# A decoder layer's mLSTM groups: row factors on GpSimd, values centred on VectorE, forget bias inside PSUM, one semaphore per tile's keys, two more banks for the experts

## The chip, the cores and the metric

The kernel runs on one core of a Trainium2 chip. The metric is the device time of one execution in microseconds (us); the time before is the median of 3 runs. All arithmetic is in float32 (large products are split into two fp32r parts).

## The reference, cut to what matters

One decoder layer works on x and ctx, each 64 sequences of 64 rows of 128 numbers: attention with a layer norm, then an mLSTM over ctx with queries from x and a layer norm, then a mixture of experts (one shared, eight routed, two of them per row) with a last norm.

```python
x = _layernorm(x + attn(x))
# mLSTM: q is x; k and v are ctx; 4 heads of 32 columns
ig = einsum('bsd,hd->bhs', concat[q, k, v], w_igate) + b_igate
fg = einsum('bsd,hd->bhs', concat[q, k, v], w_fgate) + b_fgate
log_f = jax.nn.log_sigmoid(fg)
log_D = tril(cumsum(log_f)_s - cumsum(log_f)_t) + ig_t
max_log_D = max_t(log_D)
D = exp(log_D - max_log_D)
C = (qh @ kh.T) / sqrt(32) * D
Cn = C / (maximum(abs(C.sum(-1)), exp(-max_log_D)) + 1e-6)
hst = Cn @ vh
hn = (hst - hst.mean(-1)) / sqrt(hst.var(-1) + 1e-05) * (1 + ln_weight)
x = _layernorm(x + hn)
# experts: shared + sum of the two best of eight, each gelu(x @ up) @ down, + x
x = _layernorm(x + ffn(x))
```

The heads are centred by centring the values first: each row of a head of ctx loses its mean over 32 columns, so that `hst` has mean zero.

## The kernel before, in words

The 4096 rows are 32 tiles of 128 rows (two sequences each), in 8 groups of 4 tiles (GT = 4, NG = 8). The five engines run hand-written queues, each strictly in its order, that wait for one another by semaphores. There are three phases: A (attention, to about 152 us in the profiled execution), B (mLSTM and router, `group_b` on TensorE, ScalarE and VectorE, to about 248 us), then the shared expert to about 299 us and the routed experts (25 pairs of tiles, then single ones), and a last sum and norm.

Phase B is the part that is changed. In the turn of group g the queues also hold the front of group g+1 and the back of groups g-1 and g-2:

- TensorE (L1290): a transposition for the floors of g; `qk` of tile 0 and 1 (L1211: the scores and, from `al` and `rh`, the exponents of the decay, into bank 3 or 4); the gates of g+1 (L1159, into bank 7); `centred` of g+1 (L1153: the turned context times the constant `cen`, which takes the head means away); `qk` 2, `av` 0, `qk` 3, `av` 1 and 2; the context and x of group g+2 turned (L1137, L1145); `av` 3. `qk` of tile 0 waits once for the key rows of all four tiles, `al_ok`, and for `rh`.
- ScalarE (L832): floors, two `hst` copies of g-1 (which wait for VectorE's `nrm`), `decay` of tile 0, squares, `decay` 1, two copies of queries, the gates (L684: Abs into `flog`, the biased forget gate into `fpre`, Exp, Ln), the values (L678: PSUM to `vals`), `decay` 2, two queries, `decay` 3, then `emx` and the four row factors `rh` (L694, one per head), copies of the turned context and x.
- VectorE (L1825): `score` of tile 0 (`cmat`, L1661), the head variance of g-1, the norm of g-2, `score` 1, `front_rows` of g+1 (L1595: `logf`, the scan `cumf`, `arow`), `score` 2, `front_max` (L1608: the scan `amax`, then `mrow`), the residual of g-1 (two additions, `hlw` and `res`, L1693), `score` 3, moments, and `nrm` of g (L1669), which releases ScalarE's `hst`.
- GpSimd: in the first group two of the four row factors (L574); then per group one `hlw<-hst,lnw` (L488), from group 5 on also the routed rows' indirect DMAs (`scatter`, L496).
- SyncE's queue: after `arow` of a group four small DMAs (L335, `keys`) put the row of each tile into `al`; all four count on `al_ok`. Behind them stands the load of a context group into the one buffer `cs` (L324).

In the routed experts the up products of a pair of tiles go to banks 2 and 3 (L1412), which ScalarE's two Gelus (L937) must have read before the next pair's products.

## Time and profile before

| what | us |
|---|---|
| median of 3 runs | 464.09 (463.42 to 466.31) |
| the profiled execution's own time | 463.78 |
| its span, first to last instruction | 462.0 |
| TensorE busy | 437.0 (95%) |
| VectorE busy | 304.1 (66%) |
| ScalarE busy | 303.3 (66%) |
| GpSimd busy | 184.3 (40%) |

A row of a timeline has the start in us from the span's start, the length in us, the engine, the line, the operation with output<-input, shapes, the number of merged instructions, and in brackets the engine's idle time before it and what released it. With several merged instructions the length is that of all. In rows of stretches each engine has its busy us and its number of instructions; the last three numbers are TensorE's granted clock (1.00 is 2.4 GHz, 0.50 is 1.2 GHz), the DMA share and GB/s. PE is TensorE, PEld its weight load, ACT ScalarE, DVE VectorE, POOL GpSimd, SPq SyncE's DMA queue.

### The profile page before, as it was taken

How to read it: one execution, taken by the hardware profiler on the slowest of the kernel's cores; microseconds unless marked ns; L12 is line 12 of the kernel's file. 1: busy time of each engine (PE TensorE's matmuls, PEld its weight loads, DVE VectorE, ACT ScalarE, POOL GpSimd, SP SyncE). 2: the span in 40 equal slices, each digit the busy share in tenths (PEclk: the TensorE clock that was granted, in tenths of full speed). 3: DMA queues.
4: the chain of work that ended last, by engine and by line, in shares of the span. 5: the costliest groups of instructions: out<-in, count | busy, mean ns of one | idle time of the engine just before them, and what ended most of it. 6: DMA issues, size and time to landing. Idle time of an engine off the chain costs nothing.

```text
span 462.0 us, 14470 instructions
## 1 busy us (share of the span) xinstructions
PE 437.0 (95%) x5114; PEld 371.2 (80%) x5115; DVE 304.1 (66%) x965; ACT 303.3 (66%) x675; POOL 184.3 (40%) x209
## 2 busy tenths in 40 slices
PE   8999999999988999999978999999999999999993
PEld 7688888888877777677645999989998999999631
DVE  5578888888888457887867677644444444555155
ACT  4678677876766799998748974456665664233236
POOL 5621122024501011115655765637777666554300
PEclk9999999999999899999979999999999999999998
DMA  4352322900000007102212143302333332311287
GB/s 140 86 145 54 94 67 78 257 23 4 2 26 25 2 27 250 50 26 71 65 34 74 47 111 88 87 25 73 86 88 86 92 86 82 82 53 36 67 294 215
DMA packets 47710, 38.11 MB, mean 82 GB/s; under 512 B 5168, under 2 KB 41008, under 8 KB 47648
## 3 DMA queue, kind: packets, MB, share of 16 engines
q1 hardware_dynamic: 42896, 28.16, 22.2%
q0 software_dynamic: 4320, 8.92, 5.8%
q8 instruction: 40, 0.66, 0.6%
q14 instruction: 22, 0.18, 0.2%
q10 hardware_dynamic: 432, 0.20, 0.1%
HBM read 19.30 MB, written 16.34 MB: 77 GB/s over the span
## 4 chain that ended last, share of the span: by engine, by line
PE 54%; DVE 17%; ACT 11%; issue 8%; DMA 6%; POOL 3%; SPq 1%; DVEq 1%; ACTq 0%; POOLq 0%
PE bank L1347 6%; PE bank L1433 6%; PE bank L1391 4%; PE bank L1401 4%; POOL routed L605 2%; DVE negmax L1565 2%; DVE prob L1562 2%; PE bank L1068 2%; PE bank L1015 2%; PE bank L1017 2%; PE bank L1016 2%; PE bank L1058 2%; PE bank L1420 2%; DVE tkr L1556 2%; PE bank L1421 2%
## 5 line engine op out<-in xcount | busy, mean ns | idle before, releaser
L605 POOL DMA_INDIRECT routed<-rh,zbuf x71 | 72.2, 1017 | 44.3 <-DVE rh L1940 28.8
L1940 DVE TENSOR_SCALAR rh<-bank,zbuf 128x128 f32<-128x128 f32 x71 | 24.8, 350 | 39.8 <-PE bank L1433 21.5
L1433 PE MATMUL bank<-wdn,prob 128*128 x400 | 49.5, 276 | 0.6 <-DVE rh L1940 0.4
L1433 PEld LDWEIGHTS bank<-wdn,prob 128*128 128x128 f32 x400 | 47.0, 192 | 1.4 <-DVE rh L1940 1.1
L502 POOL DMA_INDIRECT slots<-zbuf,slot x32 | 32.7, 1021 | 22.0 <-PE bank L1347 5.4
L940 ACT ACTIVATE prob<-bank 128x512 f32<-128x512 f32 x50 | 29.8, 597 | 13.7 <-PE bank L1422 10.8
L502 POOL DMA_INDIRECT slots<-tkr,slot x32 | 31.1, 972 | 13.8 <-issue 5.7
L492 POOL TENSOR_TENSOR hlw<-hst,lnw 128x512 f32<-128x512 f32 x8 | 10.3, 1284 | 59.1 <-ACT hst L815 59.1
L925 ACT ACTIVATE prob<-bank 128x512 f32<-128x512 f32 x21 | 12.5, 597 | 29.2 <-PE bank L1391 29.2
L1420 PE MATMUL bank<-xT_hi,wq_hi 128*128 128x256 f32 x100 | 30.3, 303 | 0.9 <-DVE xT_lo L1950 0.9
L1347 PEld LDWEIGHTS bank<-sdn,qblk 128*128 128x128 f32 x256 | 29.6, 192 | 0.5
L638 ACT ACTIVATE prob<-prob 128x512 f32<-128x512 f32 x32 | 20.2, 631 | 14.7 <-DVE prob L1566 14.6
L1347 PE MATMUL bank<-sdn,qblk 128*128 128x128 f32 x256 | 29.7, 275 | 0.0
L1946 DVE TENSOR_TENSOR wq_lo<-wup,wq_hi 128x512 fp32r<-128x512 f32 x25 | 17.4, 696 | 18.0 <-ACT wq_hi L931 13.0
L1421 PE MATMUL bank<-xT_hi,wq_lo 128*128 128x256 f32 x100 | 28.2, 282 | 0.0
L1422 PE MATMUL bank<-xT_lo,wq_hi 128*128 128x256 f32 x100 | 28.2, 282 | 0.0
L1015 PE MATMUL bank<-xT_hi,wq_hi 128*128 128x512 f32 x64 | 27.9, 437 | 0.0
L1224 PE MATMUL bank<-qblk,cT 128*64 128x256 f32 x128 | 22.1, 422 | 4.2 <-DMA al<-arow 4.2
L1017 PE MATMUL bank<-xT_lo,wq_hi 128*128 128x512 f32 x64 | 25.4, 397 | 0.0
L1016 PE MATMUL bank<-xT_hi,wq_lo 128*128 128x512 f32 x64 | 25.1, 392 | 0.0
L1562 DVE TENSOR_TENSOR prob<-pair,bias 128x512 f32<-128x512 f32 x32 | 22.0, 689 | 4.0 <-PE pair L1038 2.7
L1566 DVE TENSOR_TENSOR prob<-prob,negmax 128x512 f32<-128x512 f32 x32 | 23.3, 728 | 1.1
(303 smaller groups left out, 1199.4 us busy)
## 6 DMA issues: line engine op xcount, KB each, us to landing
slots<-x2T SPq DMA_DIRECT2D x8, 585.0 KB, 5.2
zbuf<-slots SPq DMA_DIRECT2D x25, 130.0 KB
tkr<-in_x SPq DMA_DIRECT2D x8, 256.0 KB, 3.0
cs<-in_ctx SPq DMA_DIRECT2D x8, 256.0 KB, 2.9
wup<-in_L_ffn_routed_up SPq DMA_DIRECT2D x1, 2048.0 KB, 9.9
zbuf<-tkr SPq DMA_DIRECT2D x8, 256.0 KB
wup<-routed SPq DMA_DIRECT2D x8, 256.0 KB, 3.6
wdn<-routed SPq DMA_DIRECT2D x8, 256.0 KB, 4.3
```

What stands on the lines that cost most here:

```text
L502: pool.indirect_dma_start(slots, bass.IndirectOffsetOnAxis(ap=slot[:, k, t:t + 1], axis=0), (tkr, tk1)[k][:, t, :], None).then_inc(scat[g ...
L605: pool.indirect_dma_start(routed, bass.IndirectOffsetOnAxis(ap=xr[n][:, :].bitcast(I32)[:, DEST:DEST + 1], axis=0), yr[n % 4][:, :], None) ...
L940: act.activation(prob[:, 2 * q + b, :], bank[2 + b][:, :], ACT.Gelu).then_inc(s["hT_ok"], 1)
L1015: mm(bank[4 + h % 2][:, :], wq_hi[:, h, :], xh[:, :], start=True, stop=False)
L1016: mm(bank[4 + h % 2][:, :], wq_lo[:, h, :], xh[:, :], start=False, stop=False)
L1017: mm(bank[4 + h % 2][:, :], wq_hi[:, h, :], xl[:, :], start=False, stop=True).then_inc(s["z_ps"], 1)
L1347: m = mm(bank[4 + g % 2][:, k * D:(k + 1) * D], shT[g % 2][:, c, k * P:(k + 1) * P], sdn[:, c, :], start=(c == 0), stop=(c == FC - 1))
L1420: mm(u, wst_hi[q][:, k], xp_hi[q], start=True, stop=False)
L1421: mm(u, wst_lo[q][:, k], xp_hi[q], start=False, stop=False)
L1422: m = mm(u, wst_hi[q][:, k], xp_lo[q], start=False, stop=True)
L1433: m = mm(bank[6 + a][:, 0:D], hTp[:, q, c // 2, c % 2, a, :], wdn[:, bass.ds(e * (FC * D) + c * D, D)], start=(c == 0), stop=(c == FC - 1))
L1562: tt(prob[:, k, :].rearrange("p (e x) -> p e x", e=2), pair[:, :, 0:256], bias[:, :, :].rearrange("p (e c) j -> p e (c j)", e=2), ALU.add) ...
```

## The change

Six things are changed, the first four in phase B:

1. Two of the four row factors `rh` of groups 1 to 4 are made by GpSimd (`rows_of`), which waits for `mrow` of the group, in place of ScalarE. Group 0 had it so already; groups 5 to 7 stay with ScalarE.
2. The forget gate's bias is a row `bf` of 128 numbers, multiplied with a row of ones into bank 7 ahead of the gates' products. ScalarE's `fpre` is gone, and `logf` reads bank 7.
3. The values of groups 1, 2 and 3 are centred by VectorE from `cs`: a sum per head (`head_sums`) and one operation into `vals` (`values_d`). TensorE's `centred` and ScalarE's `values` of these groups are gone. `cs` has two buffers.
4. Each tile's key row has its own semaphore, `al_ok[k]`, and `qk` of tile k waits for its own alone.
5. The routed experts' up products use banks 2 and 3 for even pairs and 4 and 5 for odd ones; a pair waits for the Gelus of the pair but one before it.
6. Some semaphores are merged (`stored`, `prep_ps`, `lnv_ok`), with the same orders of waits.

```diff
 def context(g):                         # SyncE
     if g > 0:
-        sp.wait_ge(s["cT_ps"], g)
-    sp.dma_start(cs[:, :, :], ctx_tok[:, g * GT:g * GT + GT, :]).then_inc(s["cs_ok"], 16)
+        sp.wait_ge(s["cs_ok"], 16 * g)
+    if g > 1:
+        sp.wait_ge(s["cT_ps"], g - 1)
+    if g - 2 in BY_DVE:
+        sp.wait_ge(s["vald_ok"], BY_DVE.index(g - 2) + 1)
+    sp.dma_start(cs[g % 2][:, :, :], ctx_tok[:, g * GT:g * GT + GT, :]).then_inc(s["cs_ok"], 16)
 def keys(g):                            # SyncE
-        sp.dma_start(al[g % 2][r, k, :, :]..., arow[r, :]).then_inc(s["al_ok"], 16)
+        sp.dma_start(al[g % 2][r, k, :, :]..., arow[r, :]).then_inc(al_ok[k], 16)
+def rows_of(g):                         # GpSimd
+    if g > 0:
+        pool.wait_ge(s["mrow_ok"], g + 1)
+    if g > 1:
+        pool.wait_ge(s["dd_ps"], GT * (g - 1))
+    for h in range(NH // 2, NH):
+        pool.tensor_scalar(rh[g % 2][:, :, h, :], amax[:, :].rearrange("p (a s) -> p a s", a=2),
+                           row[:, NH + h:NH + h + 1], row[:, h:h + 1], ALU.mult, ALU.add).then_inc(s["rh_ok"], 1)
 def gates(g):                           # ScalarE
-    act.activation(flog[:, :], bank[7][:, 0:P], ACT.Abs, bias=bf[:, 0:1]).then_inc(s["fabs_ok"], 1)
-    act.activation(fpre[:, :], bank[7][:, 0:P], ACT.Identity, bias=bf[:, 0:1])
+    act.activation(flog[:, :], bank[7][:, 0:P], ACT.Abs).then_inc(s["fabs_ok"], 1)
 def maxima(g):                          # ScalarE
-    for h in range(NH if g > 0 else NH // 2):
+    for h in range(NH if g > 4 else NH // 2):
 def gates(g):                           # TensorE
+    mm(bank[7][:, 0:P], bf[:, :], one_row[:, :], start=True, stop=False, skip_group_check=True)
 def qk(g, k):                           # TensorE
-        if g == 0:
-            pe.wait_ge(s["keys_ok"], GT)
-        else:
-            pe.wait_ge(s["al_ok"], KEYS * g)
+    if g == 0:
+        pe.wait_ge(s["keys_ok"], k + 1)
+    else:
+        pe.wait_ge(al_ok[k], 16 * g)
 def front_rows(g):                      # VectorE
-    ist(stt(logf[:, :], fpre[:, :], 0.0, flog[:, :], ALU.min, ALU.subtract))
+    ist(stt(logf[:, :], bank[7][:, 0:P], 0.0, flog[:, :], ALU.min, ALU.subtract))
+def head_sums(g):                       # VectorE, g = 1, 2, 3
+    dve.wait_ge(s["cs_ok"], 16 * (g + 1))
+    c3 = cs[g % 2][:, :, :].rearrange("p k (h d) -> p (k h) d", h=NH)
+    bst(dve.tensor_reduce(vsum[:, :], c3, AX.X, ALU.add))
+def values_d(g):
+    c3 = cs[g % 2][:, :, :].rearrange("p k (h d) -> p (k h) d", h=NH)
+    stt(vals[g % 2][...][:, :, 0:DH], spread(vsum[:, :], [P, GT * NH, DH]),
+        -1.0 / DH, c3, ALU.mult, ALU.add).then_inc(s["vald_ok"], 1)
 def up_pair(p, q):                      # TensorE
-        if c % 2 == 0 and not (isinstance(p, int) and p == 0):
-            pe.wait_ge(s["hT_ok"], 2 * p - 1 + b)
-        u = bank[2 + b][:, (c % 2) * 2 * P:(c % 2 + 1) * 2 * P]
+        if c % 2 == 0 and not (isinstance(p, int) and p < 2):
+            pe.wait_ge(s["hT_ok"], 2 * p - 3 + b)
+        u = up_bank(q, b)[:, (c % 2) * 2 * P:(c % 2 + 1) * 2 * P]    # bank[2 + 2 * q + b]
```

How the queues are moved shows at two places. The first is VectorE's queue in the turn of group 2, from the end of group 1's `nrm` on. Before:

```order
L1679 SCALAR_TENSOR_TENSOR nrm<-floor,nrm 128x16
L1666 SCALAR_TENSOR_TENSOR cmat<-bank,decay 128x256
L1689 TENSOR_REDUCE hva<-hsq 128x16
L1691 SCALAR_TENSOR_TENSOR hva<-hva,nsq 128x16
L1556 TENSOR_SCALAR tkr<-res,mv,rstd 128x128 x4
L1666 SCALAR_TENSOR_TENSOR cmat<-bank,decay 128x256
L1603 SCALAR_TENSOR_TENSOR logf<-fpre,flog 128x128
```

The same stretch of the changed kernel, where `vsum` holds the head sums of `cs`:

```order
L1704 SCALAR_TENSOR_TENSOR nrm<-floor,nrm 128x16
L1853 TENSOR_REDUCE vsum<-cs 128x16
L1691 SCALAR_TENSOR_TENSOR cmat<-bank,decay 128x256
L1714 TENSOR_REDUCE hva<-hsq 128x16
L1716 SCALAR_TENSOR_TENSOR hva<-hva,nsq 128x16
L1580 TENSOR_SCALAR tkr<-res,mv,rstd 128x128 x4
L1691 SCALAR_TENSOR_TENSOR cmat<-bank,decay 128x256
L1857 SCALAR_TENSOR_TENSOR vals<-vsum,cs 128x16x32
L1628 SCALAR_TENSOR_TENSOR logf<-bank,flog 128x128
```

The head sums stand ahead of the first `cmat`, the values ahead of `logf`. The second place is GpSimd's queue at the start of phase B, before:

```order
L575 TENSOR_SCALAR rh<-amax,row 128x2x64 x2
L492 TENSOR_TENSOR hlw<-hst,lnw 128x512 x5
L502 DMA slots<-tkr,slot 43008x130
L502 DMA slots<-zbuf,slot 43008x130
L502 DMA slots<-tkr,slot 43008x130
```

And in the changed kernel, where the first row holds the factors of groups 0 and 1:

```order
L511 TENSOR_SCALAR rh<-amax,row 128x2x64 x4
L501 TENSOR_TENSOR hlw<-hst,lnw 128x512
L511 TENSOR_SCALAR rh<-amax,row 128x2x64 x2
L501 TENSOR_TENSOR hlw<-hst,lnw 128x512
L511 TENSOR_SCALAR rh<-amax,row 128x2x64 x2
L501 TENSOR_TENSOR hlw<-hst,lnw 128x512
L511 TENSOR_SCALAR rh<-amax,row 128x2x64 x2
L501 TENSOR_TENSOR hlw<-hst,lnw 128x512 x2
L520 DMA slots<-tkr,slot 43008x130
```

Two factors of the next group now stand between two `hlw`; each pair waits for `mrow`, each `hlw` for ScalarE's `hst`.

## Rows read from the trace of the kernel before

**Rows 1.** Busy time of each engine in three stretches (columns in the first row)

```profile
core 0: us, PE busy (x) PEld busy (x) DVE busy (x) ACT busy (x) POOL busy (x), PEclk, DMA share, GB/s
174.00:185.00 11.00, 11.00 (x161) 8.19 (x159) 8.45 (x31) 10.71 (x31) 1.29 (x1) 1.00 0.75 250
233.20:239.70 6.50, 4.53 (x18) 2.73 (x19) 3.94 (x19) 2.56 (x9) 3.36 (x4) 0.50 0.11 35
299.00:424.00 125.00, 123.12 (x1069) 121.55 (x1068) 60.15 (x154) 63.59 (x115) 80.27 (x79) 1.00 0.26 73
```

**Rows 2.** Timeline of ScalarE, groups 2 and 3: start, length, line, operation

```profile
174.62 0.39 ACT L805 ACTIVATE decay<-bank 128x256 f32<-128x256 f32 x1
...
177.54 0.37 ACT L687 ACTIVATE flog<-bank,bf 128x128 f32<-128x128 f32 x1
177.81 0.36 ACT L688 ACTIVATE fpre<-bank,bf 128x128 f32<-128x128 f32 x1
178.06 0.31 ACT L690 ACTIVATE flog<-flog 128x128 f32<-128x128 f32 x1
...
178.61 0.58 ACT L681 ACTIVATE vals<-pair 128x512 f32<-128x512 f32 x1
...
182.11 1.64 ACT L700 ACTIVATE rh<-amax,row 128x128 f32<-128x128 f32 x4
...
185.72 0.41 ACT L805 ACTIVATE decay<-bank 128x256 f32<-128x256 f32 x1
```

**Rows 3.** Timeline of VectorE, groups 2 and 3

```profile
178.81 0.29 DVE L1603 SCALAR_TENSOR_TENSOR logf<-fpre,flog 128x128 f32<-128x128 f32 x1 [0.96 <-ACT flog L692]
...
180.77 0.29 DVE L1613 TENSOR_TENSOR mrow<-cumf,amax 128x128 f32<-128x128 f32 x1
180.98 0.68 DVE L1697 TENSOR_TENSOR hlw<-hlw,hrs 128x512 f32<-128x512 f32 x1
181.70 0.69 DVE L1700 TENSOR_TENSOR res<-hlw,tkr 128x512 f32<-128x512 f32 x1
...
184.47 0.18 DVE L1679 SCALAR_TENSOR_TENSOR nrm<-floor,nrm 128x16 f32<-128x16 f32 x1
```

**Rows 4.** Timeline of TensorE, groups 2, 4 and 7

```profile
176.28 1.16 PE L1156 MATMUL pair<-cen,cT 128*128 128x128 f32 x8
...
196.18 0.65 PE L1224 MATMUL bank<-qblk,cT 128*64 128x256 f32 x4 [0.83 <-DMA al<-arow]
...
205.00 0.44 PE L1270 MATMUL bank<-cum,one_row 1*128 1x72 f32 x2
...
235.17 1.12 PE L1224 MATMUL bank<-qblk,cT 128*64 128x256 f32 x4 [2.65 <-DMA al<-arow]
```

**Rows 5.** Waits: who waited for whom, total, times, longest

```profile
PE bank L1224 <- DMA al<-arow: 4.2, 4, 2.6
```

**Rows 6.** Timeline of GpSimd, phases A and B

```profile
30.36 1.18 POOL L429 TENSOR_TENSOR tkr<-tkr,bout 128x512 f32 x1
...
112.25 1.64 POOL L472 COPY al<-ident 128x512 f32<-128x512 f32 x2
...
148.30 1.01 POOL L575 TENSOR_SCALAR rh<-amax,row 128x128 f32<-128x128 f32 x2 [6.69 <-issue]
```

**Rows 7.** Timeline of VectorE, phase A

```profile
30.57 1.52 DVE L1566 TENSOR_TENSOR prob<-prob,negmax 128x512 f32<-128x512 f32 x1
...
112.48 0.94 DVE L1566 TENSOR_TENSOR prob<-prob,negmax 128x512 f32<-128x512 f32 x1
```

**Rows 8.** Timeline of SyncE's queue: the key rows of group 7

```profile
230.10 2.92 SPq L339 DMA_DIRECT2D al<-arow  x4
```

**Rows 9.** Timeline of ScalarE, group 7

```profile
235.34 0.66 ACT L815 ACTIVATE hst<-bank 128x256 f32<-128x256 f32 x2 [2.44 <-DVE nrm L1679]
237.18 0.38 ACT L805 ACTIVATE decay<-bank 128x256 f32<-128x256 f32 x1 [1.18 <-PE bank L1227]
...
241.98 0.38 ACT L805 ACTIVATE decay<-bank 128x256 f32<-128x256 f32 x1 [1.75 <-PE bank L1227]
```

More of the change, by code:

```diff
@@ L146, in decoder_layer @@
     rstd = sb("rstd", [P, GT])
-    cs = sb("cs", [P, GT, D])
+    cs = [sb(f"cs{n}", [P, GT, D]) for n in range(2)]
+    vsum = sb("vsum", [P, GT * NH])
     x1T = sb("x1T", [P, W])
@@ L154, in decoder_layer @@
     vals = [sb(f"vals{n}", [P, GT, NH, DH + 1]) for n in range(2)]
-    fpre = sb("fpre", [P, P])
     flog = sb("flog", [P, P])
@@ L254, in decoder_layer @@
     scat = [sem(f"scat{n}") for n in range(NR)]
+    al_ok = [sem(f"al_ok{k}") for k in range(GT)]
     def g4(t):
@@ L573, in _ @@
         pool.wait_ge(s["mask_ok"], N_MASK)
-        for h in range(NH // 2, NH):
-            pool.tensor_scalar(rh[0][:, :, h, :], amax[:, :].rearrange("p (a s) -> p a s", a=2),
-                               row[:, NH + h:NH + h + 1], row[:, h:h + 1], ALU.mult, ALU.add).then_inc(s["rh_ok"], 1)
-        for g in range(1, 5):
-            weighted(g - 1)
+        rows_of(0)
+        for g in range(5):
+            if g > 0:
+                weighted(g - 1)
+            if g < 4:
+                rows_of(g + 1)
         in_sixth()
@@ L852, in group_b @@
                 gates(g + 1)
-                values(g + 1)
+                if g + 1 in BY_PE:
+                    values(g + 1)
             if before:
@@ L1168, in gates @@
                         m = mm(bank[7][k * HR:(k + 1) * HR, ty * P:(ty + 1) * P], wg[n][:, ty, :], src[:, k * P:(k + 1) * P],
-                               start=(n == 0), stop=(n == 1), skip_group_check=True)
+                               start=(n == 0 and ty == 1), stop=(n == 1), skip_group_check=True)
             m.then_inc(s["g_ps"], 1)
@@ L1827, in group_b @@
             placed, chosen = g >= 4 and g % 2 == 0, g >= 3 and g % 2 == 1
+            if g > 0 and g + 1 in BY_DVE:
+                head_sums(g + 1)
             if now:
@@ L1837, in group_b @@
                 score(g, 1)
+            if g == 0:
+                head_sums(1)
+            if g + 1 in BY_DVE:
+                values_d(g + 1)
             if placed:
```

87 lines of the change are left out of this document (48 added, 39 removed).

## The prediction

> **What bounds the kernel now.** I read the busy time by stretches first, then the timelines of three engines over one group of phase B, then the waits. In the routed experts, 299 to 424 us, TensorE is busy 123.1 of 125 us at full clock [rows 1]: nothing but fewer TensorE instructions helps there, and the change removes none. In phase B the reader is to see two full engines at once: from 174 to 185 us TensorE is busy 11.0 of 11 us and ScalarE 10.7, VectorE 8.5 [rows 1]. But busy is not the chain. Follow the loop from one `decay` of tile 0 to that of the next group: ScalarE starts it at 174.62 and has the gates' last operation, the Ln into `flog`, behind it when the values start at 178.61; VectorE was idle 0.96 us for that, starts `logf` at 178.81 and then has no gap until `nrm` ends at 184.65 [rows 2, 3]; `nrm` releases two `hst` copies (0.66 us for such a pair [rows 9]), then the next `decay`, at 185.3 at the earliest. It started at 185.72 [rows 2]. So the loop through ScalarE's first third and VectorE's last two thirds takes 10.7 us and the real turn 11.1: whatever is taken off TensorE or off ScalarE's last third in groups 1 to 3 can give back 0.4 us a group at most.
>
> The other thing to see is group 7: TensorE stood idle 2.65 us for the key rows and then ran at 1.2 GHz (granted clock 0.50 from 233.2 to 239.7 us, busy 4.5 of 6.5 us) [rows 1, 4]. All such waits for key rows together are 4.2 us in 4 groups [rows 5].
>
> **The change part by part.** The sum is made against the profiled execution's own 463.78 us, 0.3 under the median of the runs, 464.09; its span is 462.0. A measurement tells about 1% (4.6 us) from no change.
>
> *Less on ScalarE.* Each group loses `fpre`. Its place is 0.25 us (178.06 - 177.81), but the Exp behind it needs the Abs complete (0.37 + 0.03), so 0.12 remains [rows 2]; this lies on the loop, in all 7 groups whose front is in phase B. Groups 1 to 4 lose half of 1.64 us of `rh`, 0.8; groups 1 to 3 lose `vals`, 0.5 to 0.6 [rows 2]. Both stand behind the Ln, so off the loop of groups 1 to 3. Only in the turn of group 0, where no `hst` of an earlier group exists, ScalarE's own queue sets when group 1 starts. There 0.12 + 0.8 = 0.9 counts; the 0.5 of the values ends in a wait for `mrow`, which comes 0.1 earlier only. Term: -0.9.
>
> *Less and more on TensorE.* `centred` is 1.16 us, three times [rows 4]. The bias product is new in 8 groups; the nearest row is the other product of one row of weights, two instructions with 72 columns, 0.44 together [rows 4]; with 128 columns 0.1 to 0.4 each, I take 0.15, since a lone small product overlaps its neighbours. TensorE gains 3.5 and loses 1.2, but in groups 1 to 3 it then only waits for the `cmat` of tile 3. Term: 0, with -0.4 to +0.4 as its ends.
>
> *More on VectorE.* `head_sums` and `values_d` are 512 columns wide each, as `hlw`, 0.68 [rows 3], 3 times 1.4 us. The head sums stand where VectorE waits for the first `decay` (nrm ends 184.65, the `decay` row starts 185.72), the values where it waits 0.96 us for `flog` [rows 2, 3]. Both covers hold by 0.3 us or so in group 2, more in groups 0 and 1. If the covers went, 0.3 to 0.7 a group. `logf` from PSUM in place of SBUF: 0 to 0.1. Term: 0.
>
> *GpSimd beside VectorE.* The two factors take 1.01 us [rows 6], ready well before `qk` needs them. But they are released by `mrow`, and exactly then VectorE runs `hlw` and `res`, which read two SBUF tiles each [rows 3]. Such an addition, normally 0.69, took 1.52 us at 30.57, when GpSimd's addition ran from 30.36 to 31.54: it waited for its end. At 112.48 it took 0.94 between two GpSimd copies (112.25, 1.64 for both): it waited for the first and got in ahead of the second [rows 6, 7]. So I expect `hlw` to start first, the first factor to wait for it, `res` to wait for that factor (0.5), and the second factor to wait for `res`: +0.45 in each of groups 1 to 3, in the middle of the loop. From both sides: 0 if GpSimd comes late, 1.0 if both factors go first. In group 0 no `res` exists. With -0.12 from `fpre` that is +0.33 a group, and the slack of 0.4 hides part of it: +0.2 a group. Term: +0.6. In groups 4 to 6 only `fpre` counts, less the slower `logf`: -0.2.
>
> The Trainium skill, "SBUF — State Buffer", section "Who interferes with whom", says that a VectorE instruction with two SBUF inputs and a GpSimd one that reads SBUF exclude each other, and the second to start blocks until the first is through. By that rule the 1.4 us that look free on VectorE are joined by a stall on it; the two rows above agree, 1.52 against 0.69. Without the rule, taking the engines as independent, this term would be -0.4 in place of +0.6.
>
> *A semaphore per tile.* In group 7 the four key DMAs were issued over 2.92 us from 230.10 on, 0.73 apart, and TensorE started at 235.17 when the last had landed [rows 4, 8]. Tile 0's row is 3 x 0.73 = 2.2 us earlier, at about 233.0; the row factors are ready by then. So the idle stretch is about 0.5 us. What is late next is ScalarE: `nrm` and `hst` end at 236.0, so `decay` 0 starts there and not at 237.18: -1.2 [rows 9]. But TensorE, which stood behind with two `qk` and two shared up products at 1.2 GHz, is ahead by more: the third `qk` was needed for the `decay` at 241.98, for which ScalarE had waited 1.75 us [rows 9]. If the clock stays at 2.4 GHz, that `decay` starts when ScalarE has done the work ahead of it: 1.2 for the earlier start and the 1.75 of the wait, 2.9 us, and up to 3.5 where shorter waits inside go too. If the clock falls all the same (it had by 233.2, 0.7 us after the idle time began [rows 1, 4]), TensorE does the same work at the same speed from 2.2 us earlier on: 2.0. Everything to 248 us hangs on it, then TensorE is full. I take -2.6. In groups 1, 4 and 5 the wait for keys was 1.6 us together, 4.2 less 2.6 [rows 5], but there `nrm` comes just as late: 0, at most -0.5.
>
> *Banks.* In 125 us of the experts TensorE is idle 1.9 [rows 1], and between a pair's Gelus and the next up products stands the down product. Term: 0, at most -0.3. The doubled `cs` only loads earlier.
>
> Sum: -0.9 + 0.6 - 0.2 - 2.6 = -3.1, so 460.7 for the profiled execution and 461.0 as a median.
>
> **The rivals.**
> *Nothing blocks, and the clock holds.* GpSimd comes late or between: groups 1 to 3 give 0.4 each (-1.2 in place of +0.6), group 7 gives 3.5: -0.9 - 1.2 - 0.2 - 3.5 = -5.8, 458.3. For it: TensorE and ScalarE lose work in just these groups. Against: `mrow` releases the factors at the worst moment.
> *Both factors block, the clock falls.* 1.0 a group, less 0.12 and part of the slack: +2.1 in place of +0.6; group 7 gives 2.0: -1.0, 463.1. For it: the two factors are queued back to back, and the clock fell at 233.2 after little idle time.
> *The key rows don't come apart.* The rows are 2 KB each, and only the issue is known to be spread. If all four land together near 235, group 7 keeps its wait and the sum is -0.5: 463.6. Then the change doesn't do what it says. Against: four DMAs with 0.73 between issues.
> *The clock falls in phase B (slower).* TensorE, full in groups 1 to 3, gets gaps of about 1 us a group where dense products stood. A stretch of 6.5 us at 1.2 GHz, as in rows 1, does in 6.5 what takes 3.3: the group pays 3.3 less its 1 us of gap, 2.3. One such stretch leaves -0.8; from two on the kernel is slower: +1.5, 465.6. Against: the wait of 0.83 us in group 4 [rows 4] was followed by products at full speed.
>
> **How the numbers follow.** The forecast 0.52, the fast rival 0.14, both block 0.17, keys together 0.09, clock falls 0.08. The forecast's own range is 459.7 to 462.3. For 8 in 10 I go from 458.4 to 464.2, which leaves out part of the fast rival and nearly all of the slow one. Faster by over 1% means under 459.45: most of the fast rival and the forecast's lower edge, 0.18. Slower by over 1% means over 468.7: 0.02. Within 1%: 0.80.
>
> **What would show it.** In the profile after: TensorE's wait for `al` under 1 us in all, and in group 7 `decay` 0 right behind `hst`; the `res` addition of groups 1 to 3 at about 1.1 us in place of 0.69, and if it stays at 0.69 my blocking term is wrong; the start of `decay` 0 of group 1 about 0.9 earlier, of group 4 about 0.3 earlier; the experts' stretch as long as before. The forecast is wrong if the clock falls in groups 1 to 4, if the head sums delay the first `cmat`, or if the time of group 7 is given back before 299 us.

## The result, and the profile after

The changed kernel took 459.81 us in the median of 8 runs (456.49 to 463.35), the kernel before, run beside it, 464.37 (461.76 to 466.31, 8 runs). The medians lie 4.6 us or 1.0% apart. The ratio, which is formed over the fast runs and is not that of the two medians, is 0.9916, with a 95% interval from 0.9888 to 0.9943, or 0.8% faster. Both stand at the edge of the 1% that such a measurement tells apart by itself. The forecast was 461.0. The profiled execution took 460.13 us with a span of 458.1, against a span of 462.0 before: 3.9 us less by the spans (3.65 by the executions' own times, 463.78 and 460.13), where the sum said 3.1.

The first part of the page of the changed kernel (busy us, share of the span, number of instructions):

```profile
PE 436.4 (95%) x5106; PEld 370.1 (81%) x5107; DVE 307.1 (67%) x971; ACT 297.7 (65%) x656; POOL 190.1 (42%) x217
```

TensorE's busy time is nearly what it was (437.0 before). The three products `centred` are gone, eight bias products have come, and idle time was lost. Busy time by stretches, for group 2 (decay 0 to decay 0), the stretch at 1.2 GHz, and the routed experts:

```profile
core 0: us, PE busy (x) PEld busy (x) DVE busy (x) ACT busy (x) POOL busy (x), PEclk, DMA share, GB/s
173.31:183.73 10.42, 10.34 (x155) 7.53 (x153) 9.27 (x32) 9.67 (x30) 2.95 (x3) 1.00 0.70 244
229.60:236.20 6.60, 6.44 (x37) 4.09 (x34) 5.25 (x25) 4.04 (x15) 5.25 (x5) 0.50 0.11 34
299.00:424.00 125.00, 122.86 (x1074) 122.04 (x1073) 59.69 (x157) 64.82 (x117) 80.55 (x79) 1.00 0.25 72
```

Beside [rows 1] the reader is to see three things. Group 2 lasts 10.42 us and no longer 11.1, and ScalarE is a little less full (9.67 of 10.42 us busy, 10.71 of 11 before). The clock still falls in group 7: 0.50 from 229.6 to 236.2, only that TensorE now works through it (6.44 of 6.6 us busy, where it was 4.53 of 6.5). The experts are as before, 122.86 of 125 us.

Timeline of ScalarE, groups 2, 3 and 7, which answers to [rows 2, 9]:

```profile
173.31 0.39 ACT L823 ACTIVATE decay<-bank 128x256 f32<-128x256 f32 x1
...
180.13 0.87 ACT L718 ACTIVATE rh<-amax,row 128x128 f32<-128x128 f32 x2
...
183.73 0.39 ACT L823 ACTIVATE decay<-bank 128x256 f32<-128x256 f32 x1
...
233.19 0.66 ACT L833 ACTIVATE hst<-bank 128x256 f32<-128x256 f32 x2 [2.19 <-DVE nrm L1704]
233.74 0.39 ACT L823 ACTIVATE decay<-bank 128x256 f32<-128x256 f32 x1
...
238.06 0.38 ACT L823 ACTIVATE decay<-bank 128x256 f32<-128x256 f32 x1 [1.96 <-PE bank L1249]
```

Two factors stand where four did (0.87 us for 1.64), and in group 7 decay 0 now follows `hst` at once. Timeline of VectorE in group 2, which answers to [rows 3]:

```profile
172.65 0.68 DVE L1853 TENSOR_REDUCE vsum<-cs 128x16 f32<-128x512 f32 x1
173.79 0.42 DVE L1691 SCALAR_TENSOR_TENSOR cmat<-bank,decay 128x256 f32<-128x256 f32 x1 [0.46 <-DVE vsum L1853]
...
176.46 0.68 DVE L1857 SCALAR_TENSOR_TENSOR vals<-vsum,cs 128x512 f32<-128x512 f32 x1
177.34 0.29 DVE L1628 SCALAR_TENSOR_TENSOR logf<-bank,flog 128x128 f32<-128x128 f32 x1 [0.20 <-ACT flog L710]
...
179.51 0.68 DVE L1722 TENSOR_TENSOR hlw<-hlw,hrs 128x512 f32<-128x512 f32 x1
180.23 0.82 DVE L1725 TENSOR_TENSOR res<-hlw,tkr 128x512 f32<-128x512 f32 x1
```

The head sums (0.68 us) run ahead of the first `cmat` and the values (0.68) ahead of `logf`, which then still waits 0.20 us for `flog`: the cover of 0.96 us held. The addition `res` takes 0.82 us, not 0.69. Timeline of GpSimd in the turns of groups 0, 1 and 2, which answers to [rows 6]:

```profile
160.21 0.88 POOL L511 TENSOR_SCALAR rh<-amax,row 128x128 f32<-128x128 f32 x2 [11.06 <-DVE mrow L1638]
...
169.27 1.68 POOL L511 TENSOR_SCALAR rh<-amax,row 128x128 f32<-128x128 f32 x2 [4.50 <-DVE mrow L1638]
...
179.69 1.68 POOL L511 TENSOR_SCALAR rh<-amax,row 128x128 f32<-128x128 f32 x2 [4.92 <-DVE mrow L1638]
```

The same two factors take 0.88 us at 160.21 and 1.68 us at 169.27 and 179.69, where VectorE runs its two additions. Timeline of TensorE in the turn of group 6 and at the start of group 7 (beside [rows 4]):

```profile
219.41 0.48 PE L1186 MATMUL bank<-one_row,bf 1*128 1x128 f32 x2
219.82 0.43 PE L1190 MATMUL bank<-x1T,wg 128*32 128x128 f32 x8
...
226.52 0.66 PE L1268 MATMUL bank<-vals,cmat 64*64 64x33 f32 x16 [0.55 <-issue]
...
230.94 1.12 PE L1246 MATMUL bank<-qblk,cT 128*64 128x256 f32 x4 [0.16 <-issue]
```

The bias product holds TensorE from 219.41 to 219.82, 0.41 us. The wait for the key rows, 2.65 us before, is 0.16. SyncE's queue, the key rows of groups 6 and 7 (beside [rows 8]):

```profile
213.49 2.91 SPq L348 DMA_DIRECT2D al<-arow  x4
...
227.95 2.48 SPq L348 DMA_DIRECT2D al<-arow  x4
```

Where the time went, with the stretches of both profiled executions. The mark is GpSimd's iota, which the last attention scores of phase A release; "decay 0" is ScalarE's of tile 0 of a group; the last border is the first Gelu of the routed experts.

| stretch, us | before | after | difference |
|---|---|---|---|
| to the mark | 141.41 | 141.27 | -0.14 |
| mark to decay 0 of group 1 | 23.21 | 22.07 | -1.14 |
| groups 1 to 3 | 32.68 | 31.68 | -1.00 |
| groups 4 and 5 | 24.38 | 24.60 | +0.22 |
| group 6 (to decay 0 of group 7) | 15.50 | 14.12 | -1.38 |
| group 7 and the shared expert | 67.84 | 67.36 | -0.48 |
| routed experts to the end | 157.0 | 157.0 | 0 |

### The profile page after: what moved, and what is told of

It is laid out like the page before. It is cut to its first block, busy times and chain, and to the rows that moved or that the text cites. A ratio compares the mean times of both kernels' runs of the same rounds, so it can differ in the third digit from the quotient of the medians.

```text
span 458.1 us, 14489 instructions
## 1 busy us (share of the span) xinstructions
PE 436.4 (95%) x5106; PEld 370.1 (81%) x5107; DVE 307.1 (67%) x971; ACT 297.7 (65%) x656; POOL 190.1 (42%) x217
## 4 chain that ended last, share of the span: by engine, by line
PE 62%; DVE 18%; ACT 8%; issue 5%; DMA 4%; POOL 1%; DVEq 1%; SPq 0%; ACTq 0%; POOLq 0%
PE bank L1457 9%; PE bank L1371 6%; PE bank L1415 4%; PE bank L1425 4%; PE bank L1444 2%; PE bank L1446 2%; PE bank L1445 2%; DVE negmax L1589 2%; DVE prob L1586 2%; PE bank L1087 2%; PE bank L1034 2%; PE bank L1077 2%; PE bank L1246 2%; PE bank L1036 2%; PE bank L1035 2%
## 5 line engine op out<-in xcount | busy, mean ns | idle before, releaser
L959 ACT ACTIVATE prob<-bank 128x512 f32<-128x512 f32 x50 | 29.8, 597 | 13.6 <-PE bank L1446 10.7
L944 ACT ACTIVATE prob<-bank 128x512 f32<-128x512 f32 x21 | 12.5, 598 | 29.1 <-PE bank L1415 29.1
L1268 PEld LDWEIGHTS bank<-vals,cmat 64*64 64x64 f32 x512 | 17.3, 136 | 8.9 <-issue 8.9
L432 POOL TENSOR_TENSOR xT_lo<-x1T,xT_hi 128x512 fp32r<-128x512 f32 x4 | 5.2, 1293 | 45.4 <-ACT xT_hi L644 45.4
```

The lines of the kernel that those rows point to most:

```text
L959: act.activation(prob[:, 2 * q + b, :], up_bank(q, b)[:, :], ACT.Gelu).then_inc(s["hT_ok"], 1)
```

## The experiments

Twelve kernels ran, on three chips; each is compared with the kernel before on its own chip. Single runs of one kernel scatter by 6 us and more. TensorE's clock falls to 1.2 GHz in up to four stretches of about 3 to 10 us of phase B, and which ones differs between profiles; but this is only a part of the scatter: over the 31 and 35 runs of the kernel before on the first two of these chips, time and mean granted clock go together only weakly (correlation -0.3 on each). So the medians tell parts of 0.5 us from nothing only poorly, and the parts are read from the stretches of the profiles, where a stretch at full clock repeats to 0.05 us. All rows of this table are computed from the timelines as above; "cold" are the stretches, in whole us, in which the granted clock was 0.50 between 140 and 260 us.

| kernel | mark to group 1 | groups 1-3 | 4, 5 | 6 | 7, shared | experts | cold |
|---|---|---|---|---|---|---|---|
| before | 23.21 | 32.68 | 24.38 | 15.50 | 67.84 | 157.0 | 151-154, 233-239 |
| changed | 22.07 | 31.68 | 24.60 | 14.12 | 67.36 | 157.0 | 151-154, 229-236 |
| e1, keys only | 21.57 | 32.72 | 25.41 | 14.19 | 67.45 | 158.3 | 203-210, 230-237 |
| e2, one wait | 21.13 | 31.64 | 24.57 | 14.10 | 68.81 | 157.3 | 230-233, 243-250 |
| e3, rows by ScalarE | 21.26 | 31.40 | 24.63 | 14.11 | 68.14 | 157.3 | 230-233, 244-251 |
| e4, values by TensorE | 23.16 | 32.98 | 24.41 | 14.27 | 67.97 | 157.7 | 150-154, 232-236, 246-253 |
| e7, with fillers | 20.59 | 31.66 | 24.59 | 14.13 | 65.24 | 158.7 | none |
| e9, bias undone | 20.65 | 34.48 | 25.88 | 13.52 | 65.63 | 157.6 | 170-177, 218-225, 245-249 |
| e11, values alone | 21.43 | 32.04 | 25.60 | 14.52 | 67.87 | 158.1 | 203-209, 230-237 |
| e12, values and keys | 21.40 | 34.04 | 25.92 | 13.49 | 65.61 | 157.0 | 169-176, 217-224, 244-248 |
| e13, changed again | 20.59 | 31.65 | 26.36 | 14.64 | 66.46 | 177.8 | 218-225, 246-249 |
| e5, two up banks | 20.60 | 31.65 | 26.38 | 13.59 | 68.00 | 177.9 | 217-221, 245-251 |
| e6, four by GpSimd | 20.60 | 31.66 | 26.01 | 13.87 | 68.40 | 177.1 | 218-221, 242-252 |
| e14, filler early | 20.61 | 31.65 | 28.83 | 13.95 | 68.37 | 174.8 | 204-211, 221-224, 235-238, 252-255 |

The theory at the start was the prediction's own: in groups 1 to 3 the chain of ScalarE and VectorE sets the length, GpSimd's factors cost what the lighter engines save, and the gain lies in group 7. The rival, which the profile after suggested (groups 1 to 3 shorter by 1.0, not longer by 0.6), was that TensorE sets it there and the values are the main gain.

### The key rows alone, in the kernel before (e1)

```diff
-                sp.dma_start(al[g % 2][r, k, :, :]..., arow[r, :]).then_inc(s["al_ok"], 16)
+                sp.dma_start(al[g % 2][r, k, :, :]..., arow[r, :]).then_inc(al_ok[k], 16)
-                if g == 0:
-                    pe.wait_ge(s["keys_ok"], GT)
-                else:
-                    pe.wait_ge(s["al_ok"], KEYS * g)
+            if g == 0:
+                pe.wait_ge(s["keys_ok"], k + 1)
+            else:
+                pe.wait_ge(al_ok[k], 16 * g)
```

> The kernel before with the semaphore per tile's keys alone (part 4). If the key wait of group 7 is its own gain, decay 0 of group 7 follows hst at once and this kernel is 1.5 to 2.5 us faster than before, with groups 1 to 6 within 0.5 us of it (decay 0 of group 6 near 221.7). Rival: the keys pay only together with the relief of ScalarE and TensorE in groups 1 to 3; then within 0.5 us of before. A second rival: the keys also help groups 1, 4 and 5, 1.6 us of waits, for over 3 us in all.

Measured: 462.8 us against 463.34, ratio 0.999 (0.9959 to 1.0021). In the profile group 6 is 14.19 us in place of 15.50, so decay 0 of group 7 comes 1.3 us earlier. Timeline of TensorE and of ScalarE at the start of group 7:

```profile
232.08 1.12 PE L1225 MATMUL bank<-qblk,cT 128*64 128x256 f32 x4 [0.32 <-ACT rh L701]
...
230.19 1.64 ACT L701 ACTIVATE rh<-amax,row 128x128 f32<-128x128 f32 x4
...
234.33 0.66 ACT L816 ACTIVATE hst<-bank 128x256 f32<-128x256 f32 x2 [2.35 <-DVE nrm L1681]
234.87 0.39 ACT L806 ACTIVATE decay<-bank 128x256 f32<-128x256 f32 x1
```

The key rows still took 2.92 us to issue, but `qk` waits 0.32 us for ScalarE's last factor, and `hst` and decay 0 follow `nrm`: the step of the prediction, -1.2, is confirmed at its place. In the median it shows as half a microsecond that can't be told from nothing: this profile was 1.0 us longer in groups 4 and 5, where it had a cold stretch, and 1.3 us in the experts.

### One wait for all four key rows, in the changed kernel (e2)

```diff
             if g == 0:
                 pe.wait_ge(s["keys_ok"], k + 1)
-            else:
-                pe.wait_ge(al_ok[k], 16 * g)
+            elif k == 0:
+                for j in range(GT):
+                    pe.wait_ge(al_ok[j], 16 * g)
```

> The changed kernel with one wait for all four tiles' keys ahead of qk of tile 0 (part 4 undone). Key theory: group 7 shows TensorE idle for about 2.6 us before its first qk again, decay 0 of group 7 starts 1.4 us later than in the changed kernel, and the time is 1.5 to 2.5 us above it; decay 0 of groups 1 to 6 within 0.5 us. Rival (relief theory): within 0.5 us of the changed kernel.

Measured: 462.0 us, ratio 0.9976 (0.9947 to 1.0006). But group 6 is 14.10 us, as in the changed kernel. Timelines of TensorE, of ScalarE and of SyncE's queue there:

```profile
230.31 1.12 PE L1247 MATMUL bank<-qblk,cT 128*64 128x256 f32 x4 [1.33 <-DMA al<-arow]
...
231.86 0.66 ACT L833 ACTIVATE hst<-bank 128x256 f32<-128x256 f32 x2 [2.44 <-DVE nrm L1705]
232.40 0.39 ACT L823 ACTIVATE decay<-bank 128x256 f32<-128x256 f32 x1
...
212.18 2.92 SPq L348 DMA_DIRECT2D al<-arow  x4
...
226.62 2.48 SPq L348 DMA_DIRECT2D al<-arow  x4
```

TensorE does wait 1.33 us again, yet decay 0 loses nothing, since `hst` comes just as late. The reason is the queue: in the kernels with one context buffer (before, e1) it is the key rows of group 7 that take 2.92 us to issue [rows 8], in all those with two buffers (the changed kernel and every run but e1) the ones of group 6, and group 7's take 2.48. So the 1.3 us of group 6 are had by the semaphores (e1) or without them by what moved the slow issue (e2); e11, with one wait, has 14.52. That the doubled buffer moved it goes by which kernels show it; why that one issue is slow was not tried. The 0.5 us that the semaphores do give in the changed kernel lie elsewhere: the way to group 1 is 21.13 us here and 20.59 in e7 and e13, and TensorE waited 0.48 us for the keys of group 1. The rest of the 2.2 us between the medians (462.0 and 459.8, not run side by side) is open. The intervals of the two ratios (from 0.9947 up here, up to 0.9943 there) just miss each other, but this one overlaps that of the changed kernel on the third chip (e13, 0.9923 to 0.998), and this profile doesn't show the rest to be the semaphores': it has a cold stretch from 243 to 250 us that the changed kernel's has not, and 68.81 us for group 7 and the shared expert.

### All row factors by ScalarE (e3) and all by GpSimd (e6)

```diff
-            for h in range(NH if g > 4 else NH // 2):    # ScalarE, e3
+            for h in range(NH if g > 0 else NH // 2):
-            if g < 4:                                    # GpSimd, e3
-                rows_of(g + 1)
-            for h in range(NH if g > 4 else NH // 2):    # ScalarE, e6
+            for h in range(NH if g > 4 else 0 if g > 0 else NH // 2):
-            for h in range(NH // 2, NH):                 # GpSimd, e6
+            for h in range(0 if g > 0 else NH // 2, NH):
```

> The changed kernel with all four row factors of groups 1 to 4 by ScalarE again (part 1 undone). Theory from the two traces: res was held up by 0.13 us only, not 0.45, and the factors set when ScalarE reaches the next group, so 0.8 us is lost at group 1 and up to 0.5 in each of groups 2 and 3: 1.0 to 2.0 us slower than the changed kernel. Rival (the loop through VectorE bounds, as predicted): the loss at group 1, 0.8, is given back by the missing block, 0.4 us slower at most. In both res falls from 0.82 to 0.69 us.

Measured: 460.55 us, ratio 0.9917 (0.9883 to 0.9951), the same ratio as the whole change (the medians are 0.6% apart): the rival's 0.4 us is nearer than the theory's 1 to 2. The way to group 1 is 0.67 us longer than in e7 and e13 (21.26 against 20.59), groups 1 to 3 are 0.26 shorter (31.40 against 31.66), 0.09 a group, which leaves a loss of 0.4. `res` is back at 0.69 us.

> The changed kernel with all four row factors of groups 1 to 4 on GpSimd. Theory 1 (the prediction's: a factor that gets in first blocks VectorE's addition until it ends): the res of groups 1 to 3 waits for each further factor too, 1.1 us or more in place of 0.82, and the group is longer by 0.3 to 0.5: 1 to 1.5 us slower in all. Theory 2 (each addition loses only a fixed small time, 0.13 us, and the loop hides it): res stays at 0.8 to 0.95, ScalarE loses 0.8 us a group that nobody waits for: within 0.5 us of e13_after_again, if GpSimd's later end (about 3.4 us after mrow) stays ahead of the first qk.

Measured: 482.3 us where the kernel before took 485.24 and e13 481.19, ratio 0.9974 (0.9942 to 1.0007). Timelines of VectorE and GpSimd in group 1, e6:

```profile
168.38 0.68 DVE L1722 TENSOR_TENSOR hlw<-hlw,hrs 128x512 f32<-128x512 f32 x1
169.09 0.82 DVE L1725 TENSOR_TENSOR res<-hlw,tkr 128x512 f32<-128x512 f32 x1
...
168.56 2.53 POOL L511 TENSOR_SCALAR rh<-amax,row 128x128 f32<-128x128 f32 x4 [4.65 <-DVE mrow L1638]
```

Four factors take 2.53 us, 0.85 more than two, and `res` still 0.82; groups 1 to 3 stay at 31.66. Theory 2 holds: VectorE loses 0.13 us once, however many factors stand behind. The median is 1.1 us above e13's, with overlapping intervals, and the stretches of phase B up to group 4 don't show where; its profile has more cold time (242 to 252).

### The values by TensorE, with the rest of the change (e4), and the values alone (e11)

```diff
-    BY_PE = [0, 4, 5, 6, 7]         # e4
-    BY_DVE = [1, 2, 3]
+    BY_PE = list(range(8))
+    BY_DVE = []
```

> The changed kernel with the values of groups 1 to 3 by TensorE and ScalarE again (part 3 undone, the two buffers of cs stay). Theory: the values stand off the loop, so decay 0 of group 4 moves by at most 0.5 us and the time by 0 to 0.5 us. Rival: TensorE and ScalarE were the bound of groups 1 to 3, so 1.1 us of centred a group count: 2 to 3 us slower than the changed kernel.

Measured: 464.35 us, ratio 1.0028 (1.0002 to 1.0054): without the values the change gains nothing. Groups 1 to 3 take 32.98 us, 1.3 more than in the changed kernel and even 0.3 more than before. The way to group 1 takes 23.16 us, 1.1 more than in the changed kernel and as long as before (23.21); all three profiles are cold from 151 to 154 us. Busy time in the turn of group 0, from its decay 0 to that of group 1 (PE, PEld, DVE, ACT, POOL, then the granted clock), first of e4:

```profile
154.33:164.26 9.93, 9.93 (x150) 7.19 (x148) 3.80 (x12) 8.55 (x22) 0.88 (x2) 1.00 0.11 28
```

and of the changed kernel:

```profile
154.44:163.34 8.90, 8.90 (x141) 6.22 (x139) 5.64 (x15) 7.84 (x20) 0.88 (x2) 1.00 0.03 8
```

TensorE has no gap in either, and the difference of 1.03 us is nearly one `centred`. So behind the cold stretch it is TensorE, and not ScalarE's queue, that sets when group 1 starts, and with the row factors, the keys and the bias product but without the values nothing is gained there. The opposite run keeps only the values:

```diff
-                                                         # e11, against the changed kernel
-            mm(bank[7][:, 0:P], bf[:, :], one_row[:, :], ...)
+            act.activation(fpre[:, :], bank[7][:, 0:P], ACT.Identity, bias=bf[:, 0:1])
-            if g < 4:
-                rows_of(g + 1)
-                pe.wait_ge(al_ok[k], 16 * g)             # per tile
+                    pe.wait_ge(al_ok[j], 16 * g)         # all four at tile 0
-        return bank[2 + 2 * q + b]
+        return bank[2 + b]
```

> The kernel before with the values of groups 1 to 3 centred by VectorE, and with nothing else of the change that it could feel (row factors by ScalarE, bias by ScalarE, one wait for the four key rows, two up banks). Theory 1 (the prediction's: the chain ScalarE, VectorE, nrm, hst bounds groups 1 to 3, so TensorE's 1.16 us a group are hidden): group 2, from its first decay to that of group 3, stays at 11.1 us or falls by at most 0.4; 463.4 to 464.4. Theory 2 (TensorE bounds these groups; e4_values_by_pe, the change without this part, took 464.4): the group becomes 10.95 - 1.09 = 9.9 to 10.2 us, three times 0.8 to 1.1, so 461.0 to 462.0.

Measured: 462.23 us against 462.94, ratio 0.998 (0.9946 to 1.0014). Groups 1 to 3 take 32.04 us, 0.68 less than e1, and group 2 is 10.63 in place of 11.10. Busy time in group 2, first of e4:

```profile
core 0: us, PE busy (x) PEld busy (x) DVE busy (x) ACT busy (x) POOL busy (x), PEclk, DMA share, GB/s
174.55:185.81 11.26, 11.26 (x161) 8.37 (x159) 8.91 (x30) 10.20 (x30) 3.00 (x4) 1.00 0.62 216
```

and of e11:

```profile
172.24:182.87 10.63, 10.22 (x155) 7.40 (x153) 9.27 (x32) 10.41 (x32) 1.28 (x1) 1.00 0.70 240
```

In e4 TensorE is busy all of 11.26 us: with `centred` and the bias product it is the bound, and what ScalarE and VectorE gain is lost. In e11 it has gaps, and group 2 lasts what the chain of ScalarE and VectorE was read to take, 10.7 us. So both theories were half right: TensorE bounded group 2 before, the other chain stood 0.5 us behind it, and theory 2's 9.9 to 10.2 did not come. The gain is not the same in each group: 0.47 us in group 2 (11.10 to 10.63), 0.19 in group 3 (11.58 to 11.39), none in group 1 (10.00 and 10.02). The chain became shorter only with the bias product: 31.40 us in e3, which differs from e11 by it, the keys and the banks, of which e2 excludes the keys (31.64 with and 31.66 without one wait) and the banks come later. That is 0.64 in three groups, 0.2 each, for the `fpre` that left ScalarE, with the product that came on TensorE already paid.

### Without GpSimd's rows and without the bias product (e12), and without the bias product alone (e9)

```diff
-            mm(bank[7][:, 0:P], bf[:, :], one_row[:, :], ...)             # e9 and e12
-            act.activation(flog[:, :], bank[7][:, 0:P], ACT.Abs)
+            act.activation(flog[:, :], bank[7][:, 0:P], ACT.Abs, bias=bf[:, 0:1])
+            act.activation(fpre[:, :], bank[7][:, 0:P], ACT.Identity, bias=bf[:, 0:1])
-            if g < 4:                                                     # e12
-                rows_of(g + 1)
```

> The same with a semaphore per tile's keys and the four up banks as well: the changed kernel without its GpSimd row factors and without its bias product. Theory 1: group 7 gives its 2.0 to 2.6 us, the values nothing: 461.5 to 462.0. Theory 2: the values give 2.5, the keys 0 to 0.5 and only where the clock holds: 460.5 to 461.5; group 7 stays near 14.1 us.

Measured: 460.9 us, ratio 0.9946 (0.9914 to 0.9978), in the span of theory 2; but theory 1's lies within the interval too.

> The changed kernel with the forget bias added by ScalarE again (fpre) and no bias product. Theory 1 (ScalarE's 0.12 us in the loop counts, TensorE's product is hidden): 0.12 x 7 = 0.8 us slower than the changed kernel: 460.6. Theory 2 (the product takes 0.41 us of TensorE, which bounds groups 1 to 3 and part of the others): group 2 falls from 10.42 to about 10.0, 1 to 1.5 us in all faster than the changed kernel: 458.3 to 458.8.

Measured: 459.86 us, ratio 0.992 (0.9887 to 0.9952), the same ratio as the whole change (the medians are 0.7% apart); neither theory's difference came. Both profiles have a cold stretch in group 1 or 2, and none with the bias product has one there. The idle time ahead of it, timeline of TensorE in e9:

```profile
168.16 0.66 PE L1269 MATMUL bank<-vals,cmat 64*64 64x33 f32 x16 [0.54 <-issue]
...
170.78 1.07 PE L1269 MATMUL bank<-vals,cmat 64*64 64x33 f32 x16 [0.95 <-DVE cmat L1692]
```

The changed kernel has no gap at the first of these places and 0.94 us at the second. That the missing product lets the clock fall is not shown: e11 has no such product either, has gaps of 0.49 and 0.81 us at these places, and kept the full clock in groups 1 to 3, as the kernel before and e1 did. Groups 1 to 3 of e9 took 34.48 us, 2.8 more than the changed kernel, with some 7 us at 1.2 GHz among them: so what the product costs TensorE at full clock in these groups can't be read from this run, and stays open. Nothing was changed in the experts, and e9 is no better than the changed kernel: no version beat it beyond its interval.

### Fillers against the fall of the clock (e7 and e14)

```diff
                 av(g, 1)                               # e7
+                if g == 6:
+                    pe.wait_ge(s["hsq_ok"], 2 * g)
+                    for _ in range(5):
+                        mm(bank[6][:, 3 * P:4 * P], ident[:, :], ident[:, :], start=True, stop=True)
                 av(g, 2)
```

> The changed kernel with five extra 128x128 products into an unread part of bank 6 in group 6, behind the wait of TensorE for hst that left it idle 0.55 us at 226 us, 3 us before its clock was at 1.2 GHz. They add no arithmetic that is used. Theory of the clock (idle time at 226 us lowers it, and that costs group 7 its gain from the key rows): the granted clock stays at 1.00 through group 7, which falls from 14.1 to about 12.5 us, less 0.5 to 1 for the five products: 458.5. Rival (the clock falls for another reason, or these products come too late to fill the gap): clock 0.50 from 230 us as before, and 0.5 to 1 us slower: 460.5.

Measured: 461.14 us, ratio 0.994 (0.9906 to 0.9974). Its profile has no cold stretch in phase B at all. Busy time in group 7, and TensorE in the experts:

```profile
core 0: us, PE busy (x) PEld busy (x) DVE busy (x) ACT busy (x) POOL busy (x), PEclk, DMA share, GB/s
229.60:236.20 6.60, 6.05 (x64) 3.95 (x61) 5.28 (x27) 4.10 (x15) 5.38 (x6) 1.00 0.11 33
...
337.43 1.16 PE L1461 MATMUL bank<-wdn,prob 128*128 x8 [1.60 <-DVE rh L1985]
...
349.76 1.16 PE L1461 MATMUL bank<-wdn,prob 128*128 x8 [1.75 <-DVE rh L1985]
```

Group 7 and the shared expert take 65.24 us, 2.1 less than in the changed kernel's profile: an estimate of what its cold stretch costs, from one profile of each. Group 6 is unchanged at 14.13, so the 12.5 us of the expectation were wrong: decay 0 of group 7 hangs on `nrm`, not on the clock. And against the 2.1 us stand 1.7 more in the experts (158.7 us for 157.0), where TensorE waited 1.60 us at 337.43 and 1.75 at 349.76 for VectorE's `rh`, which waited for GpSimd's indirect DMAs. That the fillers held the clock is not shown: e13, without them, was at full clock from 226 to 245 us too, and the median did not fall.

```diff
         proj(NG - 1, 2)                                # e14
+        filler(4, 6)
         out_turn(NG - 1, 3)
         turn_x(1)
         proj(NG - 1, 3)
-        filler(4, 3)
```

> The changed kernel with six products without use (three that stood behind the attention's last projection and three more) put ahead of TensorE's last wait of phase A, where it stood idle 1.33 us at 148.5 us and its clock then fell in three of ten profiles. Same arithmetic. Theory of the clock (the idle time lowers it in some executions, and that costs group 0 1.2 us): no stretch at 1.2 GHz at 151 to 154, first decay 12.3 us behind GpSimd's iota in place of 13.2, and 0.3 to 1 us less in the median than e13_after_again. Rival (where the clock falls is chance, or it then falls elsewhere): no difference in the median.

Measured: 481.34 us, ratio 0.994 (0.9909 to 0.9972); e13 beside it 481.19 and 0.9951. The idle 1.33 us are filled, the first decay comes 12.28 us behind the mark, but so it does in e13 (12.26) and in every profile without the cold stretch at 151. Later in phase B it had four cold stretches, e13 two. The rival holds.

### The change again (e13) and two up banks (e5)

> The changed kernel, unaltered, so that the three runs beside it have a neighbour on the same chip. Both theories: 0.990 to 0.993 of the kernel before. Where its clock falls may differ: of the stretches at 1.2 GHz that its first profile showed (151 to 154 and 229 to 236 us) some may be gone and others there; if they are the same two, the place belongs to the kernel, if not, much of the scatter of single runs is chance.

Measured, on a third chip: 481.19 us where the kernel before took 485.24, ratio 0.9951 (0.9923 to 0.998): the medians are 4.05 us apart, beside 4.56 in the first measurement, and the ratio is a little above the 0.990 to 0.993 expected. The two cold stretches are others than in the first profile (218 to 225 and 246 to 249), so the places do not belong to the kernel alone. Whether chance or the chip sets them is open: e5 and e6, on the same chip as e13, have theirs at nearly the same two places.

```diff
-        return bank[2 + 2 * q + b]
+        return bank[2 + b]
-                if c % 2 == 0 and not (isinstance(p, int) and p < 2):
-                    pe.wait_ge(s["hT_ok"], 2 * p - 3 + b)
+                if c % 2 == 0 and not (isinstance(p, int) and p == 0):
+                    pe.wait_ge(s["hT_ok"], 2 * p - 1 + b)
```

> The changed kernel with the up products of all pairs in banks 2 and 3, as before. Prediction: banks worth 0, at most 0.3. Theory of the traces so far (with two banks the first four pairs took 12.2 to 12.4 us from Gelu to Gelu in three kernels, with four 11.95 to 11.96 in seven): exactly 0.3 at the start of the routed experts and nothing later, since the later pairs take 13.73 in either: so 0.3 us slower than e13_after_again, less than the interval. Rival (the banks carry a part of the gain that the key rows do not): 1 us or more slower.

Measured: 481.83 us, ratio 0.9929 (0.9895 to 0.9963), not to be told from e13. Timeline of ScalarE, the second and the third pair's Gelus, e5:

```profile
304.75 1.07 ACT L959 ACTIVATE prob<-bank 128x512 f32<-128x512 f32 x2
...
308.05 1.32 ACT L959 ACTIVATE prob<-bank 128x512 f32<-128x512 f32 x2 [0.33 <-PE bank L1446]
```

and e13:

```profile
305.57 1.08 ACT L959 ACTIVATE prob<-bank 128x512 f32<-128x512 f32 x2
...
308.49 1.31 ACT L959 ACTIVATE prob<-bank 128x512 f32<-128x512 f32 x2 [0.33 <-PE bank L1446]
```

From the second pair to the third it is 3.30 us with two banks and 2.92 with four (before 3.35, changed 2.92). That is the whole effect, once, and the experts end no earlier for it: 177.9 and 177.8 us.

## Why the prediction was right, and where its working was wrong

The forecast, 461.0 with a range from 458.4 to 464.2, held the measured 459.8, and "within 1%" was the case forecast at 0.80; 0.9916 lies in it, at its edge. The sum was 0.8 us too small by the spans of the profiled executions (0.6 by their own times), and its terms were wrong by more, in both directions. One of its own signs says so too: decay 0 of group 4 was to come 0.3 us earlier and came 2.3 earlier (195.02, before 197.30).

- *The turn of group 0: -0.9, measured -1.14.* The number is near by luck. The prediction gave it to ScalarE's queue; but both profiles have a cold stretch just before, and behind it TensorE was the bound: e4, which has all of the change but the values, took 23.16 us where the kernel before took 23.21, so nearly all of the -1.14 is the `centred` that left TensorE. The mechanism of the prediction shows only in the profiles at full clock: there the rows on GpSimd are worth 0.67 (e3), the bias 0.06 (e9), and the per-tile keys 0.54 (e2), for which the prediction had 0, at most 0.5 in groups 1, 4 and 5 together. They help mostly together: from 21.43 us with neither (e11) the keys alone make 21.40 (e12), the rows with the bias product 21.13 (e2), all 20.6. How long the kernel before takes there at full clock no profile shows; the nearest, e1, took 21.57.
- *TensorE less `centred`: 0, with -0.4 to +0.4 as ends.* This is the term that failed. The reading "the loop takes 10.7 us and the turn 11.1, whatever is taken off TensorE can give back 0.4 us a group at most" was nearly right: 11.10 became 10.63 with the values alone (e11), three groups -0.64. But the term was then set at 0, and the 0.4 spent on GpSimd's blocking. Beside the rest of the change the values are worth 1.3 us in these groups (e4), because there the bias product had made TensorE the bound by more, and 1.1 in the turn of group 0.
- *The bias product: 0.15 us, from 0.1 to 0.4. It takes 0.41 to 0.42* to the start of the next product, just above the upper end, and nearly what the nearest row, 0.44 [rows 4], had said; that a small product would overlap its neighbours was an argument without a row.
- *`fpre`: -0.12 a group; measured -0.2 in groups 1 to 3* (e11 against e3): nearer to its place of 0.25 than to the 0.12 that remained beside the Exp. Then the chain is about 10.4 us, and group 2 took 10.42.
- *GpSimd beside VectorE: +0.45 a group. Measured +0.13 in `res`, +0.09 in the group.* Order and place were right (`hlw` first, the factors behind it), the size was not. The rows at 30.57 and 112.48 [rows 6, 7] had VectorE wait for a GpSimd instruction already under way; here GpSimd came second and paid: its two factors took 1.68 us for 0.88. By the Trainium skill, "SBUF — State Buffer", section "Who interferes with whom", whichever comes second blocks until the other is through. For GpSimd the trace agrees in direction, not in size: 0.8 us more, where waiting out the rest of `hlw` (0.50) and all of `res` (0.69) would be 1.2. For `res`, which that rule would have let wait for a whole factor (0.44, half of 0.88), the measurement does not bear it out: 0.13, and no more with four factors behind (e6). This term and the values together were +0.6 and came out as -1.00: groups 1 to 3 went the way of the first rival, nothing blocks, which had -1.2.
- *Groups 4 to 6, -0.2: measured +0.22 in groups 4 and 5.* The sign was wrong. These groups have the bias product and keep `centred`. That the product is the cause is not shown: e9 and e12, without it, were cold there, and e4, which has it, took 24.41, only 0.03 more than before. The cause stays open.
- *Group 7: -2.6. Measured -1.38 to decay 0 and -0.48 behind it, -1.86.* To decay 0 the working held (-1.2, right behind `hst`, which set it). Of the two branches the second came: the clock fell all the same, for which the prediction had 2.0. At full clock it would be some 2.1 more (e7), 4.0 in all where the other branch had up to 3.5. The cause it named is only one of two: in the kernel before, the semaphores give the 1.3 us (e1); in the changed one they are not needed for it (e2), as the slow issue of the key rows lies in another group.
- *Banks: 0, at most -0.3. Measured 0.4 once, at the second pair, and 0 in the end.*
- *The rival "the key rows don't come apart"* fell: TensorE waits 0.16 us. *"The clock falls in phase B"* did not come in the changed kernel's groups 1 to 4 in either of its profiles; it did in group 1 of e9 and e12 and in group 4 of e1, e11 and e14.

So the total was near partly by luck: groups 1 to 3 came out 1.6 us better than forecast, group 7 0.7 worse and groups 4 and 5 0.4 worse; the rest, 0.2 better in the turn of group 0 and 0.1 ahead of the mark, leaves the 0.8. The step that failed inside a right total is the reading that TensorE's relief is hidden.

## What to carry to other kernels

Where two chains are within half a microsecond of each other, take the relief off both: in groups 1 to 3 the values alone gave 0.6 to 0.7 us, the lighter ScalarE with the bias product but without the values (e4) nothing, both together 1.0 to 1.3. Price a new small product at what the nearest like one takes in the trace, not at what overlap might leave. And before crediting a semaphore with a wait, look at what else moved the transfer: one run that adds it alone and one that removes it alone gave different answers here.
